# Heads of queries and keys expand in four transfers of 72 rows per batch, instead of twelve of 24

## The reference

```
a   = layernorm(x) * ln_w + ln_b
q,k,v = a @ wq[h], a @ wk[h], a @ wv[h]            # 16 heads of 8 columns
w   = softmax(q k^T / sqrt(8) + causal mask)       # per head, 256 x 256
x1  = layernorm(x + (concat_h(w v) @ wo + x))
out = layernorm(x1 + x1 @ (W + up_aux @ lora_up @ lora_down @ down_aux)^T + b)
```

## Time and profile before

| | |
|---|---|
| median of 3 runs | 437.6 us (436.97 to 439.66) |
| the profiled execution | 438.39 us |
| its span | 436.7 us |
| PE busy, share of the span | 418.1 us, 96% |
| DVE, ACT, POOL busy | 381.4, 342.1, 308.0 us |
| DMA packets, bytes | 77915, 69.16 MB |

### The profile page before, as it was taken

How to read it: one execution, slowest core, us unless ns; L and a number is a source line. 1 busy time by engine, 2 the same in 40 slices (tenths; PEclk the granted TensorE clock), 3 DMA queues, 4 the chain that set the end, 5 groups by cost and what they waited for, 6 DMA issues and landing times.

```text
span 436.7 us, 15760 instructions
## 1 busy us (share of the span) xinstructions
PE 418.1 (96%) x5571; PEld 335.9 (77%) x5571; DVE 381.4 (87%) x1056; ACT 342.1 (78%) x865; POOL 308.0 (71%) x395
## 2 busy tenths in 40 slices
PE   7698999999999999999999999999999999998994
PEld 3366677888888888888888888888888888877762
DVE  4589978999999999999999999999999999988664
ACT  2376777788888888888888888888888888887871
POOL 6764857777777777777777778777777777754763
PEclk9699999999999999999999999999999999999998
DMA  2566576665775667666676666666676676555111
GB/s 77 151 171 170 152 190 148 164 169 155 196 192 164 180 173 175 179 174 165 176 194 176 171 166 178 173 173 169 161 193 183 170 176 175 147 140 137 42 49 38
DMA packets 77915, 69.16 MB, mean 158 GB/s; under 512 B 9307, under 2 KB 68530, under 8 KB 77874
## 3 DMA queue, kind: packets, MB, share of 16 engines
q1 hardware_dynamic: 76446, 67.68, 59.2%
q10 hardware_dynamic: 1428, 0.95, 0.9%
HBM read 47.07 MB, written 21.00 MB: 156 GB/s over the span
## 4 chain that ended last, share of the span: by engine, by line
PE 84%; DVE 5%; DMA 4%; SPq 2%; ACT 2%; issue 2%; POOL 0%; POOLq 0%; ACTq 0%; DVEq 0%
PE pv_bank L1363 20%; PE score_bank L1344 12%; PE bank L1376 11%; PE bank L1371 8%; PE max_bank L1330 7%; PE max_bank L1326 6%; PE max_bank L1331 6%; PE score_bank L1345 6%; PE bank L1433 3%; PE bank L1434 3%; DVE rowmax L1042 2%; DMA kx<-k_rows 2%; PE score_bank L1420 1%; DMA q_rows<-parts 1%; ACT qx L670 1%
## 5 line engine op out<-in xcount | busy, mean ns | idle before, releaser
L1042 DVE TENSOR_REDUCE rowmax<-max_bank 128x2 f32<-128x512 f32 (+1 forms) x384 | 245.8, 675 | 16.5 <-PE max_bank L1331 8.8
L615 ACT ACTIVATE probs<-score_bank 128x384 f32<-128x384 f32 x512 | 222.3, 491 | 39.1 <-PE score_bank L1345 26.5
L512 POOL TENSOR_SCALAR_AFFINE_SELECT probs<-probs 128x1024 f32<-128x1024 f32 x127 | 137.8, 1095 | 56.6 <-ACT probs L615 56.4
L1344 PE MATMUL score_bank<-qx,kx 74*128 74x256 bf16 x512 | 119.9, 273 | 0.5 <-DMA qx<-mT 0.5
L1345 PE MATMUL score_bank<-qx,kx 74*128 74x128 bf16 x512 | 101.6, 218 | 0.0
L1363 PE MATMUL pv_bank<-probs,v_ext 128*32 128x256 f32 x2032 | 97.5, 329 | 0.0
L1330 PE MATMUL max_bank<-kx,qx 128*128 128x128 bf16 x512 | 86.6, 221 | 2.3 <-DVE rowmax L1042 2.3
L1331 PE MATMUL max_bank<-kx,qx 74*128 74x128 bf16 x512 | 86.2, 220 | 0.0
L1363 PEld LDWEIGHTS pv_bank<-probs,v_ext 128*32 128x32 f32 x2032 | 56.3, 109 | 31.9 <-issue 6.8
L1330 PEld LDWEIGHTS max_bank<-kx,qx 128*128 128x128 bf16 x512 | 48.6, 98 | 15.0 <-issue 5.9
L1344 PEld LDWEIGHTS score_bank<-qx,kx 74*128 74x128 bf16 x512 | 49.7, 97 | 6.5 <-issue 1.6
(11 more groups left out here) (123 smaller groups left out, 615.7 us busy)
## 6 DMA issues: line engine op xcount, KB each, us to landing
kx<-k_rows SPq DMA_DIRECT2D x187, 96.0 KB
qx<-q_rows SPq DMA_DIRECT2D x128, 96.0 KB
qx<-q_rows SPq DMA_DIRECT2D x64, 104.0 KB
q_rows<-parts SPq DMA_DIRECT2D x32, 192.0 KB, 2.2
k_rows<-parts SPq DMA_DIRECT2D x31, 192.0 KB, 2.4
xa<-in_x SPq DMA_DIRECT2D x32, 128.0 KB, 3.9
xr<-in_x SPq DMA_DIRECT2D x32, 128.0 KB, 2.3
out<-y SPq DMA_DIRECT2D x32, 128.0 KB, 3.4
```

Source lines behind the costliest of these rows:

```text
L512: pool.affine_select(out=t, in_=t, compare_op=ALU.is_ge, fill=0.0, base=0, pattern=[[0, GROUP * NB], [1, P]], channel_multiplier=-1)\
L615: act.activation(probs[:, h, 0:PW], score_bank[SCORE_BANK[h]][:, 0:PW], ACT.Exp, scale=SCALE / Q_SCALE)\
L1042: dve.tensor_reduce(to, of, AX.X, ALU.max).then_inc(s_mread[unit], 1)
L1344: pe.matmul(b[:, 0:SEQ], k[0:SCORE_ROWS, i, 0:P], q[0:SCORE_ROWS, i, :], start=True, stop=True)
```

## The change

Each half of the heads (now called a set) is expanded by one transfer of queries and one of keys, of 72 rows each. Their source is a hand-made access pattern with three groups of 24 rows: the queries' groups repeat the same rows (step 0), the keys' start 8 rows apart. The rows of zeros no longer go through DRAM: `store_zero_rows` is gone, and `clear_max_rows` copies `zero_rows` from SBUF into the two rows of each batch. `load_max_rows` moves both rows in one transfer. `s_expand[0]` counts three transfers, `s_expand[1]` two. At the start ACT issues two transfers of keys instead of five, and SP none.

```diff
-        q_rows = [nc.dram_tensor(f"q_rows{i}", [(PART_ROWS + MAX_PARTS) * HEADS, SEQ], BF16).ap() for i in range(2)]
+        q_rows = [nc.dram_tensor(f"q_rows{i}", [PART_ROWS * HEADS, SEQ], BF16).ap() for i in range(2)]
...
-        EXPAND = 16 * 2 * PARTS
+        EXPAND = [16 * 3] + [16 * 2] * (SETS - 1)
...
+        def queries_of(number, parity):
+            t = q_rows[parity]
+            return bass.AP(tensor=t.tensor, offset=number * SET * SEQ,
+                           ap=[[0, PARTS], [HEADS * SEQ, PART_ROWS], [1, SET * SEQ]])
+
+        def keys_of(number, parity):
+            t = k_rows[parity]
+            return bass.AP(tensor=t.tensor, offset=number * SET * SEQ,
+                           ap=[[HD * HEADS * SEQ, PARTS], [HEADS * SEQ, PART_ROWS], [1, SET * SEQ]])
...
-            def store_zero_rows():
-                sp.wait_ge(s_zero, 1)
-                for rows_of in q_rows:
-                    sp.dma_start(rows_of[PARTS * P:, :], zero_rows[:, :]).then_inc(s_zero, 16)
...
+            def clear_max_rows(slot):
+                sp.dma_start(qx[slot][SPLIT_ROWS:SCORE_ROWS, :, :], zero_rows[:, :]).then_inc(s_expand[0], 16)
...
             def expand(it, o):
                 if it.static:
-                    sp.wait_ge(s_zero, 33)
+                    sp.wait_ge(s_zero, 1)
...
-                sp.wait_ge(s_expand[0], it.done(o - 1, EXPAND))
-                alone(sp, "sp")
-                r = it.ring(o)
-                q, k = (t[it.parity(o)].rearrange("(r h) s -> r h s", h=HEADS) for t in (q_rows, k_rows))
-                for half in range(HALVES):
-                    heads = slice(half * HALF, half * HALF + HALF)
-                    if half == 0:
+                sp.wait_ge(s_expand[0], it.done(o - 1, EXPAND[0]))
+                r, p = it.ring(o), it.parity(o)
+                clear_max_rows(r)
+                for number in range(SETS):
+                    if number == 0:
                         sp.wait_ge(s_q_stored, it.done(o, 16))
                     else:
-                        sp.wait_ge(s_expand[1], it.done(o - 1, EXPAND))
-                    for turn in range(PARTS):
-                        a, n = turn * PART_ROWS, PART_ROWS + (MAX_PARTS if turn == PARTS - 1 else 0)
-                        sp.dma_start(qx[r][a:a + n, heads, :], q[0:n, heads, :]).then_inc(s_expand[half], 16)
-                    if half == 0:
+                        sp.wait_ge(s_expand[number], it.done(o - 1, EXPAND[number]))
+                    sp.dma_start(qx[r][0:SPLIT_ROWS, heads_of(number), :], queries_of(number, p))\
+                        .then_inc(s_expand[number], 16)
+                    if number == 0:
                         sp.wait_ge(s_stored, it.done(o, STORES))
-                    for turn in range(PARTS):
-                        a = turn * PART_ROWS
-                        sp.dma_start(kx[r][a:a + PART_ROWS, heads, :],
-                                     k[turn * HD:turn * HD + PART_ROWS, heads, :]).then_inc(s_expand[half], 16)
+                    sp.dma_start(kx[r][0:SPLIT_ROWS, heads_of(number), :], keys_of(number, p))\
+                        .then_inc(s_expand[number], 16)
...
             def load_max_rows(it, o):
                 sp.wait_ge(s_mT, it.done(o))
-                for part in range(MAX_PARTS):
-                    sp.dma_start(qx[it.ring(o)][SPLIT_ROWS + part:SPLIT_ROWS + part + 1, :, :],
-                                 mT[part * HEADS:(part + 1) * HEADS, :]).then_inc(s_mrow, 16)
+                sp.dma_start(qx[it.ring(o)][SPLIT_ROWS:SCORE_ROWS, :, :], mT[:, :]).then_inc(s_mrow, 16)
```

More of the change, by code:

```diff
@@ L25 @@
 HALVES = HEADS // HALF
+SETS = 2
+SET = HEADS // SETS
 VW = P // GROUP
@@ L188, in build @@
         s_const = sem("constants_made")
-        s_zero = sem("zero_rows_made_and_stored")
+        s_zero = sem("zero_rows_made")
         s_vfill, s_ones, s_mask_made = sem("v_ext_filled"), sem("ones_made"), sem("mask_rows_made")
@@ L202, in build @@
         s_q_stored, s_stored = sem("q_stored"), sem("k_stored")
-        s_expand = sems("heads_expanded_half", HALVES)
+        s_expand = sems("heads_expanded_set", SETS)
         s_v, s_vx = sem("v_in_bank6"), sem("v_ext_ready")
@@ L226, in build, with heads_of @@
         N_MASKS = 4 + 2 * RUN
-        EXPAND = 16 * 2 * PARTS
+        EXPAND = [16 * 3] + [16 * 2] * (SETS - 1)
         STORES = 16 * 2
-        MAX_ROWS = 16 * MAX_PARTS
+        def heads_of(number):
+            return slice(number * SET, number * SET + SET)
+        def queries_of(number, parity):
[6 more added lines that the diff above has]
+                           ap=[[HD * HEADS * SEQ, PARTS], [HEADS * SEQ, PART_ROWS], [1, SET * SEQ]])
         s_passed = {e: sem(f"waits_passed_{e}") for e in ("sp", "pool", "dve")}
@@ L287, in store_parts @@
                 if it.static:
-                    sp.wait_ge(s_expand[0], it.done(o - 2, EXPAND))
-                    sp.wait_ge(s_expand[1], it.done(o - 2, EXPAND))
+                    for number in range(SETS):
+                        sp.wait_ge(s_expand[number], it.done(o - 2, EXPAND[number]))
                 p3 = it.done(o)
@@ L326, in store_first_queries @@
             def store_first_queries():
                 sp.wait_ge(s_p3q, 1)
[L328 to L347, removed]
+                sp.dma_start(q_rows[0].rearrange("(i p) s -> p i s", p=P), parts[:, :, 0, :]).then_inc(s_q_stored, 16)
+            def expand_first_queries():
+                sp.wait_ge(s_zero, 1)
+                sp.wait_ge(s_slot[0], 2)
+                clear_max_rows(0)
+                sp.wait_ge(s_q_stored, 16)
+                for number in range(SETS):
+                    sp.dma_start(qx[0][0:SPLIT_ROWS, heads_of(number), :], queries_of(number, 0))\
+                        .then_inc(s_expand[number], 16)
@@ L364, in first @@
                 load_weights()
-                store_zero_rows()
                 load_xa(at, 1)
@@ L368, in first @@
                 store_first_queries()
-                expand_first_queries(0)
-                expand_first_queries(1)
-                expand_first_keys_turn()
+                expand_first_queries()
                 load_xa(at, 3)
@@ L620, in copy_maxT @@
                 if it.static:
-                    act.wait_ge(s_mrow, it.done(o - 1, MAX_ROWS))
+                    act.wait_ge(s_mrow, it.done(o - 1, 16))
                 act.activation(mT[:, :], bank6[:, :].bitcast(BF16)[0:MAX_PARTS * HEADS, 0:SEQ], ACT.Copy)\
@@ L655, in store_first_keys, with expand_first_keys @@
                                   parts[:, 0:n, 1, :]).then_inc(s_stored, 16)
[L657 to L666, removed]
+            def expand_first_keys():
+                act.wait_ge(s_slot[0], 2)
+                act.wait_ge(s_stored, STORES)
+                for number in range(SETS):
+                    act.dma_start(kx[0][0:SPLIT_ROWS, heads_of(number), :], keys_of(number, 0))\
+                        .then_inc(s_expand[number], 16)
             def fill_queries(slot):
@@ L726, in first @@
                 copy_v(at, 0)
-                expand_first_keys(0)
-                expand_first_keys(1)
+                expand_first_keys()
                 first_parts(at, 1)
@@ L1318, in max_scores @@
                 quad, kind = unit // 3, unit % 3
-                if unit % (UNITS // HALVES) == 0:
-                    pe.wait_ge(s_expand[unit // (UNITS // HALVES)], it.done(o, EXPAND))
+                if unit % (UNITS // SETS) == 0:
+                    number = unit // (UNITS // SETS)
+                    pe.wait_ge(s_expand[number], it.done(o, EXPAND[number]))
                 pe.wait_ge(s_mread[(unit - 2) % UNITS], it.done(o if unit >= 2 else o - 1))
@@ L1338, in scores @@
                 if h == 0:
-                    pe.wait_ge(s_mrow, it.done(o, MAX_ROWS))
+                    pe.wait_ge(s_mrow, it.done(o, 16))
                 last = last_in_bank(h)
```

## The result

The changed kernel takes 690.68 us (median of 4 runs, 689.49 to 694.39), the kernel before 438.0 us (436.97 to 439.66). The ratio is 1.578, 95% interval 1.570 to 1.586. The profiled execution of the changed kernel took 690.73 us, its span is 689.0 us. Executions over 1.5% above the fastest one of the same kernel are left out of every comparison here, among them one of the kernel before that took 589.31 us at a mean granted clock of 0.656.

What follows compares the result with a forecast made beforehand. Transfers on three engines were to set the pace, PE waiting: 33.3 us start + 31 x 21.3 us rounds + 37 us tail = 730.6 us of span, plus 1.7, less 0.8, giving 731 us; range 685 to 940.

Steps and rivals of the forecast that it cites:

- lower bound of 20.5: Busiest engine's work per batch: 16.4 us expansions, 3.2 us stores, 0.9 us clearing and maxima, with no exposed gap.
- Rate, 24.0 GB/s: Each of three engines expanding queries and keys moves 24.0 GB/s, so its 393 kB take 16.4 us a batch.
- slow-engine rival: The three expansion engines do no better than 17.3 GB/s: 955 us, or 843 us halfway to the forecast; chance 0.14.
- The exposed gap, 0.8 us: Between batches, 1.5 us without queries to expand while their store lands; half of it counted, 0.8 us.
- upper bound of the working: For the gap between batches: all 1.5 us without queries to expand, made of 0.6 + 0.9 us.
- The round, 21.3 us: Steady batch on the busiest engine: 20.5 us of transfers plus 0.8 us of gap, 31 times.
- Start and end: First batch's expansion landed at 33.3 us; tail of 37 us from the last landing.
- What PE waits for: In each round PE waits 9 us, busy some 12 of 21; the chain names kx<-k_rows and qx<-q_rows.
- Half clock: In steady rounds, PE at half clock or another loop link makes a round 24 us or more; chance 0.10.
- Twelve engines: Rival: the destination's 72 rows decide, twelve engines carry them, rounds stay 12.2 us; 434.6 us, 3.0 us saved; chance 0.14.

Runs made afterwards that it cites:

- the run with ACT: The changed kernel with the maxima's transfer issued by ACT right behind the copy that makes it, not by SP: 696.99 us, ratio 1.590 to the kernel before.
- stage A: Part of a separate kernel of DRAM-to-SBUF transfers only, reference's work left out: 12 engines, 2 rows each of 24 neighbouring partitions; 13 GB/s per busy engine in its stretch.
- stage C: Part of a separate kernel of DRAM-to-SBUF transfers only, reference's work left out: 12 engines, 6 rows each of 72; 18 GB/s per busy engine in its stretch.

## Why the prediction was right

The forecast was 731 us in a range of 685 to 940, and slower at 0.86; 690.7 us lies in the range and 40 us below the forecast. The mechanism is the one forecast. The sizes are less good: a round took 20.07 us (worked out below), which is under the lower bound of 20.5 that the working gave, and the range held because its lower end had been put at a batch in 20 us. By its steps:

The bytes of four transfers on three engines at the measured rate fill most of a round, see below. (One slip on the way: an engine's 98 kB per batch before are 12 transfers of 8.2 kB; the 12.2 that stands there is the length of a round.)
- **Rate, 24.0 GB/s.** A little low: 26 GB/s in the stretch 227 to 229, and at that rate 393 kB take 15.1 us and not 16.4. (It isn't held throughout: from 204 to 205.5 it is 46 GB/s at the same share, 15 GB/s each.) The slow-engine rival (17.3 GB/s, 955 us) is out.
- **The exposed gap, 0.8 us.** There is one, and it is longer. From 216.5 to 218.5 the engines move 20 GB/s where the three alone move 80: three quarters of 2 us, 1.5 us, are lost, the upper bound of the working. Before it SP waits for the store of the queries to land (41.4 us in 27 waits, above), and after its issue at 216.29 the new expansion has hardly begun at 218.5.
- **The round, 21.3 us.** The issues of the batches 1 and 31 are 602.09 us apart (33.97, below, and 636.06), 20.07 us a round. 31 x (21.3 - 20.07) = 38 us are nearly the whole difference of 40 us. By these stretches the rate took 1.3 us off the forecast and the gap put 0.7 back, so two errors partly cancelled; where the other 0.6 us lie, in the stores, the clearing or the maxima, no stretch separates.
- **Start and end.** Close. The first expansion was to land by 33.3, and SP issues the next batch's at 33.97. The tail was to be 37 us: the maxima of batch 30, behind the last expansion, land at 647.99 + 7.13 = 655.1, which leaves 34 us of the span.
- **What PE waits for.** Half right. PE is busy for 15 of 20 us in a round, not 12 of 21. I expected the chain to name the keys and queries in every round; it names the maxima, which I had put behind the expansions for the tail alone. As the run with ACT shows, taking that wait away doesn't shorten the time: PE then waits for the keys instead, 168.1 us.
- **Half clock.** The clock did fall, to 0.50 in the stretch 217 to 219 and to 0.83 on the mean, and it cost nothing that shows: PE is busy for 432.83 of 580 us even so and then waits for the maxima, which stand behind the expansions. In the run with ACT, PE has only 6% of the chain, and the time is no shorter. From a scores' matmul of 256 columns to the next matmul it is 0.21 us in that stretch (217.55 to 217.76) and 0.11 at full clock (210.12 to 210.23); at half clock all the time a round would by that need up to 2 x 12.2 = 24.4 us of PE.
- **Twelve engines.** With another pattern the edit does run on twelve engines, in the time of the kernel before. The rival's gain of 3.0 us didn't come: it counted the saved issues and neither the clearing ahead, nor the longer issue of 72 rows, nor that a larger transfer lands as a whole.

SP's first row and the chain's row that these numbers rest on:

```profile
33.97 0.71 SPq L326 DMA_DIRECT2D qx<-q_rows  x1
```

```profile
647.99 7.13 DMA qx<-mT
```

## What to carry to other kernels

When transfers are merged, look at the leading count of both sides of the new pattern, not at the number of bytes or of issues: a count of 3 put a 72-row transfer on three of sixteen engines, and swapping two counts brought twelve back. Work out the bytes on the busiest engine per round, add the time in which a new transfer waits for a landing, and compare with the round; here 8 engines were just too few and 12 enough. And when a transfer that is small and far behind tops the chain of waits, ask what is queued ahead of it on its engines before moving it: here moving it gained nothing.

## What was not expected of the hardware

- SP's own issues take longer while its transfers stand behind full engines: two stores of the keys take 4.02 us to issue (208.01) and an output store 2.05 us (200.48), where in the kernel before it is 1.05 us and 0.40 (below). Issue time is then no longer a property of the transfer. Why SP is held was not tried.
- Issuing a 72-row transfer takes 0.7 to 0.8 us (above), one of 24 rows 0.38, so merging three saves a third of the issue time and not two thirds.
- Twelve engines with two rows each move 166 GB/s in the stretch of stage A, and 221 GB/s with six rows each in that of stage C; three engines move 80. A quarter of the engines gave 36 to 48% of the rate.

The two issues in the kernel before:

```profile
104.17 0.40 SPq L360 DMA_DIRECT2D out<-y  x1
...
120.52 1.05 SPq L296 DMA_DIRECT2D k_rows<-parts  x2
```
